# Linear attention and a mixture of experts on one core: row weights moved to ScalarE, weight splits cut into pieces, eleven shared blocks summed from PSUM

## What is computed

```python
x = x + _layernorm(_L0_attn_ref(_layernorm(x), Wq, Wk, Wv, Wo, Wg, bg))
x = x + _layernorm(_L0_ffn_ref(_layernorm(x), gate_w, ew1, ew2, ew3, sw1, sw2, sw3))

def swiglu(x, w1, w2, w3):
    h = x @ w1
    return h * jax.nn.sigmoid(h) * (x @ w2) @ w3
# _L0_ffn_ref: top 2 of 8 experts for each row, weights = softmax over the two
out = jax.vmap(one_expert, in_axes=(0, 0, 0, 2))(ew1, ew2, ew3, w).sum(0)
out = out + swiglu(x, sw1, sw2, sw3)
```

## Time and profile before

| What | us |
|---|---|
| Median of 3 runs | 860.36 |
| Lowest, highest | 857.39, 863.71 |
| Profiled execution, its own time | 861.15 |
| Its span, first to last instruction | 859.2 |
| PE busy | 740.7 (86%) |
| DVE busy | 635.4 (74%) |
| ACT busy | 415.6 (48%) |
| POOL busy | 494.2 (58%) |

### The profile page before, as it was taken

How to read it: one execution, slowest core, us unless ns; L and a number is a source line. 1 busy time by engine, 2 the same in 40 slices (tenths; PEclk the granted TensorE clock), 3 DMA queues, 4 the chain that set the end, 5 groups by cost and what they waited for, 6 DMA issues and landing times.

```text
span 859.2 us, 25434 instructions
## 1 busy us (share of the span) xinstructions
PE 740.7 (86%) x8863; PEld 612.1 (71%) x8863; DVE 635.4 (74%) x1286; ACT 415.6 (48%) x840; POOL 494.2 (58%) x653
## 2 busy tenths in 40 slices
PE   5779989899899984867597889898999999999983
PEld 4557777787787763635486778787899985688873
DVE  4897989989998992778876766667555554547996
ACT  2645667566676542222234334433554444445553
POOL 4133335887778776689413877687534434325665
PEclk8999999999999996768799999999999999999998
DMA  7434333444453437662332111211212111217885
GB/s 245 99 80 104 102 101 82 151 120 114 137 158 108 130 109 249 208 178 74 92 106 78 51 45 57 76 45 50 76 57 76 57 51 59 79 48 219 196 169 102
DMA packets 57480, 93.24 MB, mean 109 GB/s; under 512 B 7216, under 2 KB 35760, under 8 KB 57360
## 3 DMA queue, kind: packets, MB, share of 16 engines
q1 hardware_dynamic: 40512, 60.66, 24.8%
q0 software_dynamic: 10672, 22.57, 9.7%
q10 hardware_dynamic: 6176, 8.40, 3.6%
HBM read 59.60 MB, written 32.01 MB: 107 GB/s over the span
## 4 chain that ended last, share of the span: by engine, by line
PE 33%; DVE 18%; issue 5%; ACT 3%; POOL 1%; DVEq 1%; DMA 1%; ACTq 0%; POOLq 0%
PE bank L1285 19%; PE bank L1327 10%; DVE chosen L1576 4%; DVE wpart L1529 2%; PE bank L1305 2%; DVE bank L1634 2%; ACT gh L1369 2%; DVE gl L1625 1%; DVE wtmp_p L1588 1%; DVE chosen L1574 1%; PE bank L1269 1%; DVEq L1168 1%; DVE wmax L786 1%; DVE stc L1601 1%; ACT xh L1386 1%
## 5 line engine op out<-in xcount | busy, mean ns | idle before, releaser
L1285 PE MATMUL bank<-xh,W 128*128 128x256 f16 x1504 | 271.9, 282 | 47.9 <-DVE gl L1625 41.0
L1285 PE MATMUL bank<-xl,W 128*128 128x256 f16 x752 | 211.8, 282 | 1.5 <-issue 1.5
L1285 PEld LDWEIGHTS bank<-xh,W 128*128 (+1 forms) x1504 | 151.7, 101 | 76.1 <-issue 41.5
L1716 POOL DMA_INDIRECT yt_scratch<-ysh,dest x71 | 76.4, 1076 | 161.8 <-ACT ysh L1407 124.6
L1369 ACT ACTIVATE gh<-bank 128x512 f16<-128x512 f32 x103 | 61.3, 595 | 223.0 <-DVE bank L1634 214.5
L1327 PE MATMUL bank<-W,gh 128*128 (+1 forms) x824 | 141.3, 276 | 3.0 <-DVE gl L1625 1.9
L1625 DVE TENSOR_TENSOR gl<-bank,gh 128x512 f16<-128x512 f32 x103 | 71.0, 689 | 66.9 <-ACT gh L1369 66.3
L1327 PE MATMUL bank<-W,gl 128*128 (+1 forms) x412 | 113.8, 276 | 0.3 <-issue 0.3
L555 POOL DMA_INDIRECT xs_scratch<-xn_all,posi x64 | 88.5, 1382 | 27.5 <-issue 13.9
L1634 DVE SCALAR_TENSOR_TENSOR bank<-sl,w_scale,bank 128x512 f32<-128x512 f32 x94 | 70.8, 753 | 35.5 <-PE bank L1285 19.5
L607 PE MATMUL bank<-xnT,wT 128*128 128x256 f32 x384 | 94.2, 397 | 2.3 <-ACT xnT L369 2.3
(11 more groups left out here) (205 smaller groups left out, 1412.6 us busy)
## 6 DMA issues: line engine op xcount, KB each, us to landing
W<-gate_scratch SPq DMA_DIRECT2D x64, 256.0 KB
ysh<-yt_scratch SPq DMA_DIRECT2D x16, 512.0 KB, 4.6
xt<-xs_scratch SPq DMA_DIRECT2D x31, 260.0 KB
W<-in_L_ffn_ew_dram ACTq DMA_DIRECT2D x15, 512.0 KB, 3.7
W<-in_L_ffn_ew_dram SPq DMA_DIRECT2D x9, 512.0 KB, 8.3
x_in<-in_L_attn_x_dram SPq DMA_DIRECT2D x16, 256.0 KB, 3.6
out_dram<-x SPq DMA_DIRECT2D x16, 256.0 KB
xT_scratch<-xn2T SPq DMA_DIRECT2D x16, 256.0 KB
```

Source lines behind the costliest of these rows:

```text
L1285: last = mm(dst[n % 2][:, i * R:(i + 1) * R], W16[:, e, m, s, at:at + P], a[:, k, :], start=(k == 0 and s == 0 and a is x_h), stop=(k == K ...
L1716: pool.indirect_dma_start(yt_d[:, :], bass.IndirectOffsetOnAxis(ap=dest[:, j:j + 1], axis=0), ysh[:, ETILES + j % RING, :], None).then_inc ...
```

## The change

Six things change.

- `weights_of_rows` goes from DVE to ACT. There it stands at the end of an iteration, behind `high_g` of the second half, and takes four instructions for a single and five for a pair: absolute value, `relu(1 - x)`, one multiply-and-add for each tile, and the scale.
- `split` works in pieces: three products of 128 x 1024, three casts of 128 x 1024, six subtractions of 128 x 512, with waits between dependent ones.
- `BETWEEN` goes from 6 to 2.
- `EARLY` goes from 5 to 4: the first routed unit is unit 4, `T0` is 44, and 12 shared units stand behind the singles.
- Chunks 5 to 15 (eleven) are summed straight from the bank; only chunks 0 to 4 go through `ysh`. PE's `project` into that bank waits for the sum (`mix2`) in place of ACT's copy.
- The order of the chunks is 0, 5, 1, 6, 2, 7, 3, 8, 4, 9, 10 to 15: two each in units 47 to 51 (first one from `ysh`, then one from the bank), one each in units 52 to 57.

```diff
-    EARLY = 5
+    EARLY = 4
...
+        straight = {t.u + 2: t.n for t in shared[EARLY + 1:]}
+        kept = list(range(EARLY + 1))
+        order, mixes = [], {}
+        for u in range(MIX0, ENDS):
+            steps = ([kept.pop(0)] if kept and u < ENDS - 2 else []) + [straight[u]]
+            mixes[u] = list(range(len(order), len(order) + len(steps)))
+            order += steps
...
             def project(t, e):
-                if t.u >= 2:
+                if t.u >= 2 and t.u - 2 <= T0:
                     pe.wait_ge(T["yo_ready"], rows_upto(t.u - 2))
+                elif t.u >= 2:
+                    pe.wait_ge(U["mix2"], order.index(units[t.u - 2].n) + 1)
...
+            def weights_of_rows(t, e):
+
+                x, done = xt[t.q % 2], tags_upto(t.q - 1)
+                far, own, part = chosen2[:, 0, 0:t.tiles], chosen2[:, 1, 0:t.tiles], chosen2[:, 2, 0:t.tiles]
+                act.wait_ge(T["tag_ready"], done + 2)
+                need(act, T["wrow_ready"], t.q)
+                act.activation(far, tag[:, t.j:t.j + t.tiles, 1], ACT.Abs).then_inc(T["tag_ready"], 1)
+                act.wait_ge(T["tag_ready"], done + 3)
+                act.activation(own, far, ACT.Relu, scale=-1.0, bias=1.0).then_inc(T["tag_ready"], 1)
+                act.wait_ge(T["tag_ready"], done + 4)
+                for r in range(t.tiles):
+                    act.activation(part[:, r:r + 1], x[:, r, D + 3:D + 4], ACT.Identity, scale=own[:, r:r + 1],
+                                   bias=x[:, r, D + 2:D + 3]).then_inc(T["tag_ready"], 1)
+                act.wait_ge(T["tag_ready"], tags_upto(t.q))
+                act.activation(wrow[:, t.j:t.j + t.tiles], part, ACT.Copy, scale=w_scale[:, 2, e])\
+                   .then_inc(T["wrow_ready"], 1)
...
                     high_g(t, 1)
+                if following is not None and following.routed:
+                    weights_of_rows(following, e_of[u + 1])
...
-                if following is not None and following.routed:
-                    weights_of_rows(following, expert_of(dve, following))
...
-            BETWEEN = 6
+            BETWEEN = 2
...
-                pool.tensor_scalar(wtmp_p[:, :, :].rearrange("p m n -> p (m n)"), whole, w_scale[:, 1, e:e + 1], 1.0,
-                                   ALU.mult, ALU.mult).then_inc(T["pool_split"], 1)
+                for m in range(3):
+                    pool.tensor_scalar(wtmp_p[:, m, :], W[:, e, m], w_scale[:, 1, e:e + 1], 1.0,
+                                       ALU.mult, ALU.mult).then_inc(T["pool_split"], 1)
```

More of the change, by code:

```diff
@@ L1139, in rows_upto, with tags_upto @@
             return sum(t.tiles if t.routed else 1 for t in units[:u + 1])
+        def tags_upto(q):
+            return sum(4 + t.tiles for t in routed[:q + 1])
         def halves_upto(u):
@@ L1152, in projected, with from_bank @@
                     if t is not None and lag == (2 if t.kind == "single" else 1)]
-        LATE = C - EARLY
         MIX0, ENDS = T0 + 3, NUNIT + 2
-        alone = ENDS - 2 - MIX0
-        mixes = {u: [] for u in range(MIX0, ENDS)}
-        for c in range(C - 2):
-            mixes[MIX0 + c * alone // (C - 2)].append(c)
-        mixes[ENDS - 2], mixes[ENDS - 1] = [C - 2], [C - 1]
-        assert all(len(cs) in (1, 2) and c - EARLY + T0 + 2 <= u for u, cs in mixes.items() for c in cs)
+        straight = {t.u + 2: t.n for t in shared[EARLY + 1:]}
[5 more added lines that the diff above has]
+            order += steps
+        assert sorted(order) == list(range(C)) and not kept
         PLAIN = (C - 2, C - 1)
-        x1_of = {c: xt[c % 2][:, :, 0:D] for c in PLAIN}
+        x1_of = {k: xt[k % 2][:, :, 0:D] for k in PLAIN}
+        def from_bank(c):
+            return order[c] > EARLY
         def entry(eng, row, t, least, most):
@@ L1439, in scalar_b @@
                     e = e_of.pop(y.u)
-                    if y.routed or y.n not in PLAIN:
+                    if y.routed or y.n <= EARLY:
                         rows_out(y, e)
@@ L1567, in beside @@
                     scales(link, dve, spread_b[1], 2)
-            def weights_of_rows(t, e):
-                x = xt[t.q % 2]
-                own, part, out = chosen2[:, 0, 0:t.tiles], chosen2[:, 1, 0:t.tiles], wrow[:, t.j:t.j + t.tiles]
-                dve.wait_ge(T["tag_ready"], 2 * (t.q + 1))
-                link(V.tensor_scalar(own, tag[:, t.j:t.j + t.tiles, 1], 0.0, None, ALU.is_equal))
-                link(V.tensor_tensor(part, own, x[:, 0:t.tiles, D + 3], ALU.mult))
-                link(V.tensor_tensor(part, part, x[:, 0:t.tiles, D + 2], ALU.add))
-                V.tensor_scalar(out, part, w_scale[:, 2, e], None, ALU.mult).then_inc(T["wrow_ready"], 1)
             def add_rows(c):
@@ L1687, in pool_b @@
         def pool_b(pool):
-            BETWEEN = 6
+            BETWEEN = 2
             def split(e):
-                whole = W[:, e].rearrange("p m n -> p (m n)")
+                done = 11 * (e - 1)
                 if e > 1:
                     pool.wait_ge(experts_split, e - 1)
-                pool.tensor_scalar(wtmp_p[:, :, :].rearrange("p m n -> p (m n)"), whole, w_scale[:, 1, e:e + 1], 1.0,
-                                   ALU.mult, ALU.mult).then_inc(T["pool_split"], 1)
-                pool.wait_ge(T["pool_split"], 2 * e - 1)
-                settle(pool)
-                pool.tensor_copy(W16[:, e, :, 0, :], wtmp_p[:, :, :]).then_inc(T["pool_split"], 1)
-                pool.wait_ge(T["pool_split"], 2 * e)
-                pool.tensor_tensor(W16[:, e, :, 1, :], wtmp_p[:, :, :], W16[:, e, :, 0, :], ALU.subtract)\
-                    .then_inc(experts_split, 1)
+                for m in range(3):
+                    pool.tensor_scalar(wtmp_p[:, m, :], W[:, e, m], w_scale[:, 1, e:e + 1], 1.0,
+                                       ALU.mult, ALU.mult).then_inc(T["pool_split"], 1)
+                for m in range(3):
+                    pool.wait_ge(T["pool_split"], done + 3 + m)
+                    settle(pool)
+                    pool.tensor_copy(W16[:, e, m, 0, :], wtmp_p[:, m, :]).then_inc(T["pool_split"], 1)
+                for m in range(3):
+                    pool.wait_ge(T["pool_split"], done + 4 + m)
+                    for k in range(2):
+                        half = slice(k * MW // 2, (k + 1) * MW // 2)
+                        last = m == 2 and k == 1
+                        if last:
+                            pool.wait_ge(T["pool_split"], done + 11)
+                        pool.tensor_tensor(W16[:, e, m, 1, half], wtmp_p[:, m, half], W16[:, e, m, 0, half],
+                                           ALU.subtract).then_inc(experts_split if last else T["pool_split"], 1)
             def scatter(j):
-                need(pool, T["tag_ready"], 2 * (tile_unit[j].q + 1))
+                need(pool, T["tag_ready"], tags_upto(tile_unit[j].q - 1) + 2)
                 need(pool, T["dest_ready"], j)
@@ L1747, in finish @@
                 pool.wait_ge(U["lnc_ready"], B * (c + 1))
-                pool.dma_start(out_by_step[c], lnc[c % LN][:, :, :], accum_op=ALU.add)\
+                pool.dma_start(out_by_step[order[c]], lnc[c % LN][:, :, :], accum_op=ALU.add)\
                     .then_inc(out_stored[c % LN], 16)
```

19 lines of the change are left out of this document (10 added, 9 removed).

## The result

The changed kernel takes 826.06 us, the median of 4 runs (822.19 to 830.42), against 858.88 for the kernel before (4 runs, 853.3 to 863.71): a ratio of 0.962 (0.954 to 0.970). The forecast was 833.8 us with a range from 822 to 848. The profiled execution took 822.19 us, with a span of 820.2.

What follows compares the result with a forecast made beforehand. PE sets the second phase's pace; in the middle it idles for DVE, whose SBUF-only instructions POOL's hold. Middle 19.5, start 5.4 and mixing 2.5 sum to 27.4 us, from 861.15 to 833.8 us; range 822 to 848.

Steps and rivals of the forecast that it cites:

- Middle: 465 to 620 us: PE's waits for DVE (14.3 us) and its lowered clock go, 19.5 us gained, 14.3 to 21.
- To the 85th: Stretch from the 49th to the 85th start of DVE's low_g: no gain was forecast.
- Start: 380 to 462 us: gated of unit 4 comes at 414.0 in place of 419.36, 5.4 us gained, 2 to 9.5.
- Mixing: Sums at the end: about half of PE's 4.86 us idle stays, 2.5 us gained, at most 5, at worst -3.
- (1): Rival on the start: it gives nothing, 839 us; chance 18%.
- (2): Rival on mixing: sums from the bank are held as well and PE waits for them, 846 us; chance 5%.
- (3): Rival on row loading: rows load late, from weights ready 12.6 us into the pair, 865 us; chance 4%.
- (4): Rival on POOL: scatters fall behind, the ring fills and PE waits, 884 us; chance 4%.
- (5): Rival on the middle: something else keeps DVE from PE's pace and the waits stay, 853 us; chance 3%.
- the function of the absolute value: Weights on ACT: no extra table load, cost 0; over 200 us if abs were in another set.

Runs made afterwards that it cites:

- w_only: The kernel before with only the rows' weights moved to ACT (whole splits, six scatters between, five shared units first, old mixing): 826.9 us, 0.976 of before.
- p_only: The kernel before with only splits in pieces and two scatters between them, the weights left on DVE: 835.4 us, 0.986 of before.
- weights_back: The changed kernel with the rows' weights back on DVE, all else kept: 835.8 us, 0.972 of before.
- early5: The changed kernel with five shared units first in place of four, and ten sums from the bank: 818.3 us, 0.965 of before.
- swap5: The changed kernel with five shared units first and an iteration's two sums exchanged, the one from the bank first: 818.3 us, 0.952 of before.
- old_mixing: The changed kernel with sums as before, in block order, fourteen of sixteen from ysh and two from the bank: 825.2 us, 0.959 of before.
- w_long: The changed kernel with the step adding the two weights done three times on ACT, 1.3 us more a pair: 828.1 us, 0.966 of before.
- w_only_again: The kernel before with only the rows' weights moved to ACT, the same kernel as w_only measured once more, unaltered: 828.4 us, 0.962 of before.

## Why the prediction was right, and where its terms were off

The direction, the range and the mechanism held. The time was 7.7 us below the forecast, and the terms were off more than that. The lower end of the range was not what I called it: every term at its better end (21, 9.5 and 5) gives 825.7 us and not 822. The median of 826.1 lies just inside that.

**Middle: forecast 19.5, measured 20.4 and 21.9** (150.3 to 129.9 and 128.4). The working, waits plus clock, was right: 14.3 us of idle time went, as forecast, and 6.2 or 7.6 of busy time where I had 5.2. w_only and p_only show the cause: with the weights away whole splits cost nothing; with pieces in place of whole splits and the weights kept, 15.2 us are won. What cost the time were DVE's small instructions beside POOL's long ones, and each part of the change removes it without the other, wholly or for two thirds.

**To the 85th: forecast nothing, measured 1.8.** w_only gets 1.4 of it, p_only none. weights_back, with the weights back on DVE, loses 1.0. DVE's four instructions a unit also stood in the last pairs and the singles; I had called DVE idle there. The other 0.4 goes with the fifth unit: the kernels with five shared units first take 152.2 where those with four take 151.8.

**Start: forecast 5.4, measured 6.8 and 8.1.** The first split took 13.64 us where I had reckoned 15.7 (11.8 and 3 to 4 for the nine further pieces): their overhead is 0.2 us each. The rows landed 2.9 us after the issue where I had taken 3.6. From landing to `gated` of the fifth unit it took 13.9 us (395.60 to 409.53) where the working has 13.6. So the split and the landing were the terms mis-sized. The split also began 0.8 us later behind the first gated values than before (27.5 against 26.7). Together that gives 7.0, where `gated` of the fifth unit shows 7.0 and the stretch 6.8. What I did not ask matters more: I took the fifth unit as a pair for given and never priced it. early5 and swap5 (92.0 and 94.5) beside the first and second profile (102.6 and 101.3) say that it costs 7 to 11 us there, and w_only shows that the weights alone had won up to 15 (9 in its second profile). The 5.4 was a small difference of two large terms that I had not separated.

**Mixing: forecast 2.5, measured 7.1 and 4.0.** The sums from the bank are never held, 0.74 us in all eleven. I took them for held, and that was the wrong end of my range. By the rule of the Trainium skill (SBUF — State Buffer, "Who interferes with whom") that I had set beside it they are free, and the traces agree. But freeing them is not what gave the 4.0: old_mixing, with fourteen sums from `ysh`, has it too (74.4), and early5, with ten from the bank, has not (77.9). What these two share with their likes is the number of units at the end: twelve leave more of PE's time than eleven to cover the same sixteen sums. The further 3.1 is a matter of phase: the changed kernel had it in one profile of two, and all three kernels with the sums exchanged have it (71.2 to 71.3), with eleven units at the end as well as with twelve. So with that order the twelfth unit brings nothing.

**Beyond the terms.** The stretches add up to 36 us behind the first gated values, and the medians show 32.8. The kernel before was profiled once; whether that execution was a long one behind this point I can't say.

**The rivals.** (1) The start gave something. (2) Sums from the bank were not held. (3) Weights ready at 8.8 us, and w_long with 1.3 more does no harm in the middle. (4) POOL's scatters kept up: the last is issued at 729.3, and the first addition follows at 736.0. (5) The waits are gone. For the function of the absolute value the trace has no table load (the one of 1.28 us in this phase is that of the SiLU), so its cost is 0, as the Trainium skill (ScalarE: Activation LUTs, "Table sets: the hidden batching unit") has it.

## What to carry to other kernels

Where a small instruction on one engine takes as long as a big one on another, move the small one or cut the big one. Here the move alone won all 21.9 us of the middle and the cut alone 15.2; doing both paid only at the start, where the big one meets further small ones, and not in every profile. Price separately each part that fills or opens a hole, even if the diff calls it a detail: here one constant (four in place of five) cost 7 to 11 us at the start and gave 4 at the end, and nothing there once the sums were exchanged. And when two loops follow each other by semaphores, look at the order inside an iteration; exchanging two steps won 7 us with five shared units first (77.9 to 71.3), and with four it gave 71.2, where the changed kernel had shown 71.2 in one profile and 74.3 in the other.

## What the runs showed of the hardware that I had not expected

- What is held beside POOL depends on the operation as well as on where the inputs lie. TENSOR_TENSOR and TENSOR_SCALAR with all operands in SBUF are held (2.29 against 0.68; 2.98 against 0.17). BATCH_NORM_STATS2 reads SBUF alone as well and keeps its length beside an addition (0.75 us at 772.25, for two, above).
- A held instruction on 128 x 2 values ends with POOL's, so a hold is as long as what is left of that: 2.98, 2.65 and 5.83 us beside instructions of 2.83, 2.74 and 5.99. A held sum of 128 x 512 ends later: in early5 it ends at 762.40, 0.56 us behind the addition (760.10 to 761.84).
- A hold can cover several of POOL's instructions. Three products in a row, with no wait between them, hold one DVE instruction for 3.90 us (in the changed kernel, early5 and p_only).
- The scale's other instructions on 128 x 2 values in w_only_again, between the held ones, take 0.17 us: L787 at 383.90, just before a cast starts at 383.99, and L790, a RECIPROCAL, at 386.79. So one slips through where POOL's instruction waits for the one ahead. The RECIPROCAL may not need the gap: in w_only it takes 0.17 at 378.76, beside a cast that runs from 378.64 to 381.38. That a PSUM input was the cause for `gated` and `low_x` to go free was not tried by itself, since no bank was left to put the weights in.
